# Reordering around the sorted expert blocks of a two-layer kernel: first blocks turned inside the last product c, the router behind block 1, seven dense jobs among the blocks

## What is computed

```python
# layer 0
att = attention(x)                       # 16 heads, over 32 listed keys for each query (or dense)
x = x + relu((att @ Wo.T + bo) @ w1 + b1) @ w2 + b2
# layer 1
h = gelu(x @ fc1_w.T + fc1_b)            # 1024 wide
c = concat([h @ fc2_w.T + fc2_b, h @ experts_w[i].T + experts_b[i]])   # 256 wide
probs = softmax(c @ router_w.T)          # 8 experts
topk_vals, topk_idx = top_k(probs, 2)
w = topk_vals / (topk_vals.sum() + 1e-6)
x = x + sum_k((c @ expert_weights[topk_idx[k]] + topk_vals[k]) * w[k])
```

## Time and profile before

| | |
|---|---|
| device time, median of 3 runs | 522.18 us (521.99 to 524.74) |
| profiled execution | 521.58 us, span 519.6 us, mean granted clock 0.972 |
| PE busy | 473.9 us, 91% of the span, 2479 matmuls |
| PE weight loads | 325.5 us, 63% |
| DVE busy | 386.8 us, 74% |
| ACT busy | 257.9 us, 50% |
| POOL busy | 94.7 us, 18% |

### The profile page before, as it was taken

One profiled execution on the slowest core, in us unless ns is written; L12 is line 12 of the kernel. 1 busy time (PEld: TensorE's weight loads), 2 busy tenths in 40 slices (PEclk: granted clock), 3 DMA queues, 4 the chain that ended last, 5 costly groups with the idle time before them and its releaser, 6 DMA issues.

```text
span 519.6 us, 7588 instructions
## 1 busy us (share of the span) xinstructions
PE 473.9 (91%) x2479; PEld 325.5 (63%) x2479; DVE 386.8 (74%) x763; ACT 257.9 (50%) x506; POOL 94.7 (18%) x97
## 2 busy tenths in 40 slices
PE   4998889999999999898999999999999898979982
PEld 2445554444454444346888888888888687968861
DVE  4997889979879999784884788478846783624367
ACT  2016578677877775854462635262635242544300
POOL 3003101111111112000100026002600240456610
PEclk9999999999999999989999999999999989798995
DMA  7900020999300000021132201110201016253266
GB/s 227 234 0 1 1 81 0 343 304 339 108 1 0 1 1 1 0 82 51 54 69 77 88 0 68 55 42 1 82 2 42 21 62 163 67 168 124 94 212 216
DMA packets 24095, 45.25 MB, mean 87 GB/s; under 512 B 7938, under 2 KB 17794, under 8 KB 23778
## 3 DMA queue, kind: packets, MB, share of 16 engines
q1 hardware_dynamic: 21410, 37.46, 23.8%
q0 software_dynamic: 2640, 7.24, 3.9%
HBM read 35.29 MB, written 23.00 MB: 112 GB/s over the span
## 4 chain that ended last, share of the span: by engine, by line
PE 45%; DVE 4%; ACT 1%; DMA 1%; issue 1%; another core or an unknown queue 1%; SPq 0%; ACTq 0%; DVEq 0%
PE psG L1638 6%; PE psG L1640 6%; PE psG L1639 6%; PE psS L1638 5%; PE psS L1640 5%; PE psS L1639 4%; PE psO L1638 2%; PE psO L1640 2%; PE psO L1639 2%; PE psM L1638 1%; PE psM L1640 1%; PE psM L1639 1%; DVE attT L1926 1%; DMA back<-expert_results 1%; PE psM L1738 1%
## 5 line engine op out<-in xcount | busy, mean ns | idle before, releaser
L681 ACT ACTIVATE Pr<-psS 128x512 f32<-128x512 f32 x128 | 69.7, 599 | 40.7 <-PE psS L538 40.2
L758 DVE TENSOR_REDUCE few_Qa<-psG 128x2 fp32r<-128x512 f32 x116 | 74.4, 683 | 12.3 <-PE psG L523 12.3
L766 DVE SCALAR_TENSOR_TENSOR Pr<-Pr,few_W 128x1024 f32<-128x1024 f32 x64 | 79.1, 1242 | 2.8 <-ACT Pr L681 2.6
L521 PE MATMUL psG<-few_KG,QG 128*128 128x512 f32 x116 | 53.1, 498 | 3.3 <-DVE few_Qa L758 3.1
L538 PE MATMUL psS<-few_QAT,few_KP 128*128 128x512 f32 x128 | 49.5, 460 | 4.1 <-ACT Pr L681 2.4
L1878 DVE TENSOR_TENSOR hT_lo<-V,hT_hi 128x512 fp32r<-128x512 f32 x64 | 44.3, 693 | 2.2
L523 PE MATMUL psG<-Mneg,few_identb 128*128 128x512 bf16 x116 | 45.2, 390 | 0.0
L1876 DVE CAST hT_hi<-V 128x512 fp32r<-128x512 f32 x64 | 27.4, 428 | 19.6 <-ACT V L1813 11.2
L386 POOL TENSOR_TENSOR few_Qa<-Qn,few_Qa 128x256 fp32r<-128x256 f32 x16 | 18.4, 1150 | 128.9 <-ACT few_Qa L624 128.9
L538 PEld LDWEIGHTS psS<-few_QAT,few_KP 128*128 128x128 f32 x128 | 21.1, 192 | 30.4 <-issue 26.3
L1860 POOL DMA_INDIRECT expert_results<-block_out,block_rows x31 | 30.1, 972 | 40.6 <-ACT block_out L1794 32.4
(11 more groups left out here) (299 smaller groups left out, 1159.9 us busy)
## 6 DMA issues: line engine op xcount, KB each, us to landing
expert_rows<-blank_dram SPq DMA_DIRECT2D x8, 1548.0 KB, 23.6
block_rows<-expert_rows SPq DMA_DIRECT2D x31, 129.0 KB, 2.1
back<-expert_results SPq DMA_DIRECT2D x6, 512.0 KB, 6.6
staged<-w_dram SPq DMA_DIRECT2D x4, 512.0 KB, 4.5
x1T<-xT_dram SPq DMA_DIRECT2D x4, 512.0 KB, 4.4
staged<-ew_dram SPq DMA_DIRECT2D x4, 512.0 KB, 3.5
few_idxb<-entries_by_query SPq DMA_DIRECT2D x8, 192.0 KB, 6.9
out_dram<-attT SPq DMA_DIRECT2D x6, 256.0 KB, 2.7
```

The costliest lines, as they stand in the source:

```text
L521: nc.tensor.matmul(o, QG[:, (u // 2) % 2, st * P:st * P + P], self.KG[:, u % 2, 2 * p:2 * p + 2, :], start=True, stop=False)
L681: nc.scalar.activation(Pr[:, i % JOBS, 512 * f:512 * f + 512], psS[:, f, :], ACT.Exp, scale=SCALE).then_inc(self.s["s_exp"], 1)
L758: nc.vector.tensor_reduce(self.Qa[:, f % SLOTS, st, 2 * p:2 * p + 2, 48], self.guard_bank(i)[0][:, p, :].rearrange("p (h t) -> p h t", h=2 ...
L766: nc.vector.scalar_tensor_tensor(pr, pr, FMAX, self.W[:, r, :], ALU.min, ALU.mult).then_inc(self.s["s_prob"], 1)
```

## The change

It changes the order of the list and three details.

1. Chunk 3's first three gelu jobs are computed together: for half 0 of the residual the three matmuls of each of the jobs 0, 1 and 2, then the same for half 1. The wait for half 1's split moves from ahead of the first matmul to ahead of the tenth (`HALVES_FIRST`).
2. Blocks 0 to 3 are turned between c 0 and c 1 of chunk 3 (`TURNED_EARLY`).
3. The router follows sorted 1 instead of turned 4 (`ROUTER_AFTER`). The low parts of blocks 7 to 10 are made inside the router's chain on DVE (`BESIDE_ROUTER`, `low_part`).
4. Seven `experts` jobs stand among the blocks (behind blocks 7, 10, 13, 16, 19, 22, 25), 13 behind the last. `bring` comes directly behind the last block. `mix` 0 follows job 18, mixes 1 and 2 follow job 19.
5. The dense sums are kept in `crow` (one place for each of the four tiles of tokens, free once the rows are scattered) instead of the two buffers of `y`. The waits for stores of `y` go, one wait for the row scatters comes in.

```diff
-EXPERTS_AT = (9, 13, 17, 21, 25)
+TURNED_EARLY, ROUTER_AFTER = 4, 1
+EXPERTS_AT = (7, 10, 13, 16, 19, 22, 25)
+MIXED_AFTER = ((18, 0), (19, 1), (19, 2))
+BESIDE_ROUTER = (7, 8, 9, 10)
+HALVES_FIRST = 3
...
+        def summed(t):
+            return crow[:, t, 0:D]
...
-                    yield from jobs_of("c", c, range(KD), "act")
+                    yield from jobs_of("c", c, range(1), "act")
                     if c == SORTED:
-                        for i in range(BLOCKS + BLOCK_AHEAD):
+                        yield from jobs_of("turned", c, range(TURNED_EARLY), "dve")
+                    yield from jobs_of("c", c, range(1, KD), "act")
+                    if c == SORTED:
+                        for i in range(TURNED_EARLY, BLOCKS + BLOCK_AHEAD):
                             if i < BLOCKS:
                                 yield from jobs_of("turned", c, range(i, i + 1), "dve")
-                            if i == BLOCK_AHEAD - 1:
-                                yield from jobs_of("router", c, range(1), "dve")
                             if i >= BLOCK_AHEAD:
                                 yield from jobs_of("sorted", c, range(i - BLOCK_AHEAD, i - BLOCK_AHEAD + 1), "act")
+                            if i - BLOCK_AHEAD == ROUTER_AFTER:
+                                yield from jobs_of("router", c, range(1), "dve")
                             if i - BLOCK_AHEAD in EXPERTS_AT:
                                 j = EXPERTS_AT.index(i - BLOCK_AHEAD)
                                 yield from jobs_of("experts", c, range(j, j + 1), "dve")
                 else:
-                    for t in range(len(EXPERTS_AT) // 5, TT):
-                        yield from jobs_of("experts", c - 1, range(5 * t, 5 * t + 5), "dve")
-                        if t == 1:
-                            yield "bring", SORTED, 0, "", 0
-                        if t == TT - 2:
-                            yield "mix", 0, 0, "", 0
-                    for i in range(1, SORTED):
-                        yield "mix", i, 0, "", 0
+                    yield "bring", SORTED, 0, "", 0
+                    for j in range(len(EXPERTS_AT), TT * 5):
+                        yield from jobs_of("experts", c - 1, range(j, j + 1), "dve")
+                        for after, i in MIXED_AFTER:
+                            if j == after:
+                                yield "mix", i, 0, "", 0
...
+                if stage == "gelu" and i < HALVES_FIRST and c == SORTED:
+                    if i == 0:
+                        weights("fc1")
+                        for k in range(KD):
+                            pe.wait_ge(d["parts"], split_no["y", c, k])
+                            for j in range(HALVES_FIRST):
+                                mm = mm3(bank(e, n + j), parts(fc1, ALL, k, slice(j * P, j * P + P)), parts(x1, ALL, k, ALL),
+                                         k == 0, k == KD - 1)
+                                if k == KD - 1:
+                                    mm.then_inc(d["a_full"], 1)
+                    continue
...
+            def low_part(i):
+                v = number["turned", SORTED, i]
+                dve.wait_ge(d["v_full"], v + 1)
+                dve.wait_ge(d["block_hi"], i + 1)
+                nc.vector.tensor_tensor(blockT.lo[:, i % SPLIT_RING, :, :].rearrange("p k t -> p (k t)"), VBANK[v % 4][:, 0:D],
+                                        blockT.hi[:, i % SPLIT_RING, :, :].rearrange("p k t -> p (k t)").bitcast(F32),
+                                        ALU.subtract).then_inc(d["v_out"], 1)
...
                     link(nc.vector.reciprocal(rt[:, 3, :], rt[:, 2, :]))
+                    if c == SORTED:
+                        low_part(BESIDE_ROUTER[0])
                     settle()
...
                         link(nc.vector.tensor_tensor(lg[:, :, :], dl[:, :, :], hot[:, k, :, :], ALU.mult))
+                        if c == SORTED:
+                            low_part(BESIDE_ROUTER[1 + k])
                         settle()
...
                     link(nc.vector.reciprocal(rt[:, 7, :], rt[:, 6, :]))
+                    if c == SORTED:
+                        low_part(BESIDE_ROUTER[3])
                     settle()
...
                         if k == 0:
-                            dve.wait_ge(d["blocks_known"], 1)
-                            dve.wait_ge(d["tailed"], 4 * SORTED)
-                        if k >= 2:
-                            dve.wait_ge(d[f"stored{k % 2}"], 16 * (k // 2))
-                        ins = nc.vector.tensor_scalar(y[:, k % 2, :], ps[:, 0:D], pw[:, t:t + 1], None, ALU.add)
+                            dve.wait_ge(d["scattered"], 16 * 2 * TT * SORTED)
+                        ins = nc.vector.tensor_scalar(summed(t), ps[:, 0:D], pw[:, t:t + 1], None, ALU.add)
...
-                    sp.dma_start(out[t0:t0 + P, :], y[:, k % 2, :]).then_inc(d[f"stored{k % 2}"], 16)
-                    k += 1
-            for i in range(2):
-                sp.wait_ge(d[f"stored{i}"], 16 * (k // 2))
+                    sp.dma_start(out[t0:t0 + P, :], summed(i // 5)).then_inc(d["stored"], 16)
+            sp.wait_ge(d["stored"], 16 * TT)
```

20 lines of the change are left out of this document (9 added, 11 removed).

## The result

The changed kernel takes 514.53 us (median of 4, 514.05 to 515.83), the kernel before in the same measurement 523.46 (521.99 to 524.74): a ratio of 0.9836 [0.9808, 0.9864]. The forecast was 516.5, range 512 to 521. The profiled execution of the changed kernel has a span of 512.6 against 519.62.

What follows compares the result with a forecast made beforehand. The end was taken to hang on when PE gives DVE its last dense jobs, and the mixing behind them. Stage ends summed to span 513.9, time 515.9, plus 0.6 to the median's scale: 516.5 us, range 512.0 to 521.0.

Steps and rivals of the forecast that it cites:

- Part 1: Hole before chunk 3's first gelu matmul: halves fill 2.04 of 2.36, c half 0 ends 3.7 us earlier (bounds 2.0 and 3.7).
- Part 2: Turns between halves of c: PE waits for rows until 432.3, half clock loses 1.6; net 0.1 us gained of 3.7.
- rival (a): Both low-clock stretches, second half of c (1.6) and blocks (1.7), stay away: 513.2 us; chance 0.17.
- Part 3: Router behind block 1: the 1.43 wait goes, block 0 starts near 439.9 not 444.10, ACT waits before Exp; nothing more taken.
- Part 4: Block stage with seven dense jobs: terms sum to 46.9 us from 439.6, blocks end at 486.5 against 489.1.
- Rival (b): Holds, not PE's work, set the block stage's length; two jobs come on top, blocks end 491.9: 521.7 us; chance 0.16.
- Part 5: Results brought back at 493.5 not 498.58: 3.9 us by the earlier last scatter, 1.2 by the store no longer before it.
- Part 6: Tail: job 18 summed at 501.9, mix 0 to 504.4, mixes 1 and 2 to 510.3, 3.43 behind: span 513.9.
- (c): Transfers of results end last: last scatter stays at 494.92, last data at 508.9, 517.4 us; chance 0.12.
- The 9.2: Bringing results back: a documentation-based estimate of 9.2 us for 3.1 MB, 2.3 less than the trace.
- (d): Slower: a new hole at 429.5 and small matmuls with pauses keep PE at half clock through the blocks; chance 0.08.

## Why the prediction was right, point by point

**Size and sign.** Forecast 515.9 for the profiled execution by a span of 513.9; the span is 512.6. The steps missed by more than that 1.3, in both directions: block 0 started 2.7 sooner than forecast, the blocks took 1.9 less, and 3.4 of that was lost again in the tail. That the total came so close is luck in part. The medians moved more than the profiles, 523.46 to 514.53, 8.9, where 5.7 was forecast; with a fourth run the kernel before has a median 1.3 above the 522.18 that the forecast started from.

**Part 1, halves: right.** c half 0 at 423.89, forecast 424.0. From the beginning of the hole to c half 0 it was 14.93 and is 11.50: 3.4 gained, forecast 3.7. The rest to 3.8 is that this execution came to the hole 0.4 sooner, which is chance, and the missing 0.3 is the wait that is left before the second half (0.30), which I had put at nothing. On the third chip, where the hole had no low clock behind it, the same distance shrinks by 1.8 (13.32 to 11.48), just under the lower bound of 2.0. DVE kept up, as assumed.

**Part 2, early turns: the step that failed.** I took the row loads to go out at 428.28 as before ("nothing in the change makes them earlier"), and 1.6 of half clock behind the wait. They went out at 427.00. Of these 1.28, 0.7 is an earlier start of the last four row scatters (418.97 for 419.65), 0.2 their length (4.42 for 4.60), and 0.4 the landing (2.70 behind the end of the last for 3.10). The earlier start comes from the four scatters ahead of them: the third of those took 1.50 in the kernel before and 0.97 here. PE waited about 1.15 instead of 2.0, the clock stayed up, and c half 1 was over at 436.85 instead of 439.35. I named exactly this as what would show the step wrong ("row loads issued before 428"), and rival (a) covers it in part. The mechanism is real, as the execution of the kernel with five jobs shows; what I had wrong is to take the two lost scatters of my one trace as given, and that half clock must follow (it did in one of three). As for the stretch of a scatter, the rule cited there names a contention that the traces have, but not who loses by it: besides the scatter at 422.81, which takes 1.49 behind a subtraction started at 422.77, the scatters at 420.26 and 421.54 start 0.04 behind one too and take 0.97, while their subtractions take 0.77 instead of 0.69. I had looked at the last four scatters only and put 0.2 on closer splits; of all eight, two were stretched in both traces of the kernel before, and one, none and one in the three of the changed kernel. Six further executions with the same order up to there had one or two, so fewer is not shown to be the change's doing.

**Part 3, router behind block 1: right in kind.** Block 0 starts 0.35 behind the start of turned blocks 4 and 5, evictions of blocks 0 and 1 leave ahead of Exp, ACT stands 1.76 before it, and PE doesn't notice. Everything comes 2.7 sooner than forecast, by part 2. What I had not seen is a second wait: in the kernel with the router first, low parts stand behind its chain on DVE and cost PE 1.78 in the blocks, where the kernel before on the third chip has 0.41.

**Part 4, the blocks: right sum of its own terms.** Forecast 46.9 long; measured 45.0. The low clock is 1.7, as forecast (3.4 us at 0.51, from 452.4). Waits are 4.2 (45.00 less 40.81) where I let them come as they were, 5.4; the holds came four times and once behind Exp, as I had let them. Work at full clock is 39.1 (40.81 less 1.7) where I summed 39.8. In that sum one term is mis-sized: "two jobs 2.8" counts two products, but job 5 is a pair of transposes, and by the kernel with five jobs the two are 1.6; the other terms are 0.5 short. Rival (b) said that the holds would keep the stage at its length; it is 45.0 again, but as a sum of 3.8 more work, 2.6 less low clock and 1.2 less waits, and not because the holds filled up. The rival's own 491.9 is the old end of the blocks plus 2.8; a stage of 45.0 and 2.8 more from 439.6 would have ended at 487.4.

**Part 5, bring: right mechanism.** Last scatter at 488.68, bring at 491.30, 2.6 behind it (forecast 2.5), and 2.2 sooner than forecast, since the blocks are over sooner. But where there are no pauses it is worth nothing in itself: with bring in its old place it goes out at the same time, and the plain stores show that bring 4.0 earlier brings no gain. On the first chip no run says it; its traces have bring 3.66 behind the last scatter before and 2.62 after, so 1.0 of the 1.2 that I gave to the store.

**Part 6, the tail: mis-sized.** By my own terms job 18 leaves PE 14.3 behind the last block, at 496.4, and is summed at 497.5. It was summed at 500.91, 3.4 later: PE's results for jobs 7 to 9 came late to DVE, and then DVE, with sums of 1.03 one after another from 491.32, could not take it back before mix 0. I had given holds to the blocks alone. Of the 4.3 by which the blocks were over sooner than forecast (486.5 to 482.2) 3.4 was lost again here. On the third chip, where nothing comes late, mix 0 starts 15.3 behind the blocks, as summed (14.3 and 1.1). The last step, mix 0 late and mixes 1 and 2 back to back on DVE, is right: 500.91, 504.34, 4.88, and 3.4 behind. On the third chip this place of mix 0 is worth 2.6.

**Rivals.** (a) named the result of part 2 but not of the blocks, where one low stretch stayed. (c) did not come: no mix of the changed kernel waits for data, and bring 4.0 earlier changes nothing; with nine jobs it shows by 0.31. The 9.2 beside it takes a fit that the section cited there gives for one DMA of GpSimd's queue; here six go out on SyncE's, one behind the other, and the trace has 11.5. (d) did not show: clock 0.96 in the blocks.

## What to carry over

Work that an engine can do while it would wait is worth its whole time and the clock that the wait costs, and only if its own inputs are there: ask for each moved instruction when its data lands, how near that is to the edge, and how much that moment moves from one execution to the next. Putting a small step with a long chain on another engine (a router) behind the first bulk jobs took away two waits here, its own and that of what queues behind its chain. A merge of late data belongs behind the last job that feeds the same engine, and once that engine has no pause left, earlier data is worth nothing. And a term that is counted in jobs should be counted in instructions first: two jobs were one product and two transposes.

## What the runs showed of the hardware

**Pauses on one chip.** On the first chip both kernels show pauses of 2.0 to 2.8 us about every sixth result scatter (every fifth or sixth in the changed kernel), and TensorE's results seem to reach ScalarE and VectorE in bursts: block 7, whose matmuls start at 445.7, is evicted at 451.58 (the profile doesn't name what ended that wait), and job 7, whose last matmul starts at 483.23, is read at 485.59, on TensorE's signal. On three other chips none of the ten profiled executions with scatters, the same two kernels among them, has such a pause outside the wait for Exp; the changed kernel's block stage takes 37.3 to 37.6 us instead of 45.0, and the kernel before 510.6 to 510.9 instead of 522 to 523.5. No other kernel ran on the first chip, so whether they come with the chip or with the time at which it was used is open. The Trainium skill ("SBUF — State Buffer", section "Who interferes with whom") says that TensorE and ScalarE never wait on anyone; it says so of the ports of SBUF, and no run here shows whether these pauses have to do with a port. What holds the signals is not known: the pauses could not be brought about or taken away on the other chips.

**Clock.** The same hole ahead of the first gelu matmul (2.4) had about 3.4 us at half clock (1.2 GHz) behind it in the kernel before on the first chip and in the kernel without halves, and none in the kernel before on the third. A stretch of 2.90 in which TensorE was busy 1.46 had it, one of 3.00 with 1.51 in another kernel did not. Behind a wait of 1.43 before the turned blocks the kernel before was at half clock for 6.9 us on the first chip and for 3.4 on the third (441.70 to 445.10), the kernel without early turns not at all. So a wait of this size is a chance of losing 1.7 or more, and a forecast should price it as one.

**Two engines on one pair of inputs.** GpSimd needs 4.78 us for two additions of 128 x 1024 for which VectorE needs 2.48. Where the two overlapped, from 494.64 to 495.79, VectorE's first addition took 2.23 instead of 1.22, and its four 5.88 instead of 4.88. The same section of the Trainium skill says that a Vector instruction with two SBUF inputs contends with a GpSimd instruction that reads SBUF; this trace agrees, with 1.0 us. Against an indirect scatter the loss can fall on either: of 34 scatters that started 0.04 to 0.05 us behind such a subtraction, 17 took 1.49 instead of 0.97, and in the other 17 cases the subtraction took 0.77 instead of 0.69.

**Issue of DMAs on GpSimd.** An indirect scatter of 128 rows holds the queue 0.97 and 0.30 between two, a plain store of the same block 0.54 and 0.18.
